# Two-layer graph kernel: ACT copies Wh from two PSUM banks, s is spread by TensorE, the masks of the first row group come ahead of the next products

## Chip, core and metric

One core of a Trainium2 chip runs the whole kernel in one launch. The metric is device time in microseconds; the median of three runs is compared.

## The reference

x is 8192x128, adj is 8192x8192 int32 of zeros and ones. Cut to what matters:

```python
Wh = x @ W;  s = Wh @ a1;  t = Wh @ a2            # layer 0: graph attention
e = s[:, None] + t[None, :]
e = where(e > 0, e, 0.2 * e);  e = where(adj > 0, e, -9e15)
x = layernorm(x + elu(softmax(e, axis=1) @ Wh))
x1 = adj @ x / adj.sum(axis=1)                    # layer 1: mean over neighbours
out = layernorm(x + concat([x1, x], 1) @ weight + bias)
```

## The kernel before

The 8192 rows are worked in 32 groups of 256 rows; two groups share one row block of 512 rows. The 8192 columns are 64 tiles of 128; 16 tiles are a chunk (four chunks to a group), 8 tiles are a half, and a half is one buffer of masks. The exponential of the leaky sum splits into a product of a row factor and a column factor, one pair for a positive sum and one for a negative sum, so that a group is two masked matmul sums: mask bits times `factors`, where `factors` holds per tile the column factor times Wh, as a float16 high part and a float16 rest.

**Start.** `turn_x(k)` on TensorE transposes four tiles of x, ACT copies them out of PSUM (`copy_turned`, L407), `make_wh(k)` (L563) multiplies by W and by the two vectors, so that Wh, s and t of four tiles land in two PSUM banks, two tiles in each. VectorE empties the banks (`copy_wh(k)`, L773: one copy of Wh and one of s and t per bank) and reduces the largest |Wh| (`largest_wh`, L784). There are sixteen such steps. Then TensorE transposes s and t (L601), ACT copies them, SyncE stores them to DRAM and reads s back, spread over the 128 partitions, for groups 0 and 1 (`load_s`, L238). VectorE and GpSimd find the maxima that scale the factors.

**Adjacency.** GpSimd's queue loads one chunk of 512 rows by 2048 columns per transfer (`load_adj`, L352); a buffer comes free when TensorE has packed it. `pack_bits(c)` (L583) packs 16 tiles into 16-bit words by 64 small matmuls, and ACT copies the words out (`copy_words`).

**Group 0.** It makes the factors as it goes. Per chunk VectorE makes two products (`make_product`, L828: column factor times Wh, one for each sign), ACT rounds each to float16 (L474, the high part), VectorE subtracts for the rest (`low_of`, L917) and makes the masks (`masks`, L880: four `unpack` instructions, two `negative`, two `positive`, from ACT's `scores`). VectorE's order by chunk is: rests of this chunk, products of the next chunk, masks of this chunk (L1039 to L1045). ACT's order by chunk is: two high parts, words, 16 scores (L471 to L484). `scores` is one instruction per tile of 128 columns. TensorE packs chunk c+1 and then multiplies the two halves of chunk c (`multiply`, L607), 32 matmuls each.

**Later groups.** TensorE multiplies from masks that VectorE and ACT make ahead. A group's first matmul waits until VectorE has scaled the sums of the group before out of PSUM (`add_negative`, L926, which comes with the masks of the second chunk). VectorE also joins the tiles of the next row block (`join`, L854), so that fewer matmuls pack them.

**Between the layers.** Every engine reads the flag `wide_flag` into a register (`is_wide`, L229) and jumps over a body that these inputs don't need; TensorE does so at L657, between the last group and the first block of layer 1. Layer 1 multiplies the whole adjacency from `words` once more.

Of the kernel before, what the change touches and what calls it, by code (L numbers as in the profile page):

```python
# [32 lines left out]
P = 128  # L33
BITS = 16
WPT = P // BITS
TPG = 2
# [22 lines left out]
def adj_resnorm_kernel(nc, x, adj, w0, a0, w1, b1, consts, out):  # L59
# [21 lines left out]
    with ctx:  # L81
# [73 lines left out]
        acc = [ctx.enter_context(nc.psum_tensor(f"acc{k}", [P, 512], F32)) for k in range(2 * TPG)]  # L155
# [7 lines left out]
        s_row_in = [sem("s_row_in0"), sem("s_row_in1")]  # L163
        rows_in, rows1_in = sem("rows_in"), [sem("rows1_in0"), sem("rows1_in1")]
# [67 lines left out]

        block = ctx.enter_context(nc.Block())
# [3 lines left out]
        def _(sp):  # L237
# [23 lines left out]
            load_s(0, 0)  # L261
            load_s(1, 1)
# [138 lines left out]
        def _(act):  # L401
# [19 lines left out]
            copy_turned(0)  # L421
            for k in range(1, NX):
                copy_turned(k)
            act.wait_ge(s_turned, 1)
# [6 lines left out]
            act.wait_ge(t_big_ok, 1)  # L431

            def scores(g, slot, h, first=False):

                if not (first and h < MASK_SLOTS):
                    act.wait_ge(mask_used, 8 * g + h + 1)
                    act.sem_inc(slot_free, 1)
# [16 lines left out]
            def group(g, slot, loads, next_words, before_last=None, second=False):  # L454

                act.wait_ge(s_row_in[slot], 16 * loads)
                for h in range(8):
                    scores(g, slot, h)
                    if second and h == UPG + 1:
                        act.wait_ge(wh_saved, 1)  # L460
                        act.wait_ge(e_low_ok, UPG)
                        act.wait_ge(f_low_ok, UPG)
# [8 lines left out]
            for c in range(UPG):  # L471
                for k in range(2):
                    act.wait_ge(product_ok, 2 * c + k + 1)
                    act.activation(factors[:, k, c * UNIT:(c + 1) * UNIT, 0:F], product[:, (2 * c + k) % 3, :, :],  # L474
                                   ACT.Copy)\
                        .then_inc(high_ok, 1)
                if c == 0:
                    act.wait_ge(s_row_in[0], 16)
                if c == 0:
                    copy_words(0, 0)  # L480
                for h in (2 * c, 2 * c + 1):
                    scores(0, 0, h, True)
                if c < UPG - 1:
                    copy_words(0, c + 1)  # L484
                if c == 0:
                    act.wait_ge(uy_ok, 2)
                    act.activation(u_col, uy_col, ACT.Exp).then_inc(exp_cols_ok, 1)
                    act.activation(v_col, vy_col, ACT.Exp).then_inc(exp_cols_ok, 1)
            group(1, 1, 1, {3: (1, 0)}, second=True)
            group(2, 0, 2, {0: (1, 1), 1: (1, 2), 3: (1, 3)}, before_last=True)  # L490
            group(3, 1, 2, {0: (2, 0), 1: (2, 1), 3: (2, 2)})
            with act.Fori(2, NR - 1) as n:
                group(PAIR * n, 0, n + 1, {1: (n, 3), 3: (n + 1, 0)})
                group(PAIR * n + 1, 1, n + 1, {1: (n + 1, 1), 3: (n + 1, 2)})
            group(NG - 2, 0, NR, {1: (NR - 1, 3)})
            group(NG - 1, 1, NR, {})
# [44 lines left out]
        def _(pe):  # L541
# [21 lines left out]
            def make_wh(k):  # L563

                pe.wait_ge(x_t_ok, k + 1)
                if k >= 2:
                    pe.wait_ge(wh_ok, k - 1)
                for j in range(XB):
                    o = (j % 2) * (F + 2)
                    m = pe.matmul(acc[2 * (k % 2) + j // 2][:, o:o + F + 2], x_t[:, k % 2, j * P:(j + 1) * P], wq,  # L570
# [12 lines left out]
            def pack_bits(c):  # L583

                pe.wait_ge(adj_in[c], 16)
                if c >= 2:
# [20 lines left out]
            def multiply(g, h, factors_in=False, first=False, pack_chunk=None):  # L607
# [3 lines left out]
                for a in range(2 * TPG):  # L611
                    b, neg = a // 2, a % 2
                    if factors_in and a < 2:
                        pe.wait_ge((e_low_ok, f_low_ok)[neg], h // 2 + 1)
# [25 lines left out]

            pe.wait_ge(den_hi_ok, 4)
            pe.wait_ge(edge_col_ok, 1)
            for c in range(UPG):
                if c < UPG - 1:
                    pack_bits(c + 1)
                for h in (2 * c, 2 * c + 1):
                    multiply(0, h, h % 2 == 0, True)
# [9 lines left out]
            with pe.If(is_wide(pe) > 0):  # L657
# [98 lines left out]
        def _(dve):  # L756
# [16 lines left out]
            def copy_wh(k):  # L773

                dve.wait_ge(wh_made, k + 1)
                j0 = XB * k
                for half in range(2):
                    bank = acc[2 * (k % 2) + half][:, 0:2 * (F + 2)].rearrange("p (j f) -> p j f", j=2)
                    dve.tensor_copy(wh[:, j0 + 2 * half:j0 + 2 * half + 2, :], bank[:, :, 0:F])  # L779
                    d = dve.tensor_copy(cols[:, 0:2, j0 + 2 * half:j0 + 2 * half + 2],  # L780
                                        bank[:, :, F:F + 2].rearrange("p j k -> p k j"))
                d.then_inc(wh_ok, 1)

            def largest_wh(k):  # L784

                dve.wait_ge(wh_ok, k + 1)
                dve.tensor_reduce(wh_top[:, k:k + 1], wh[:, XB * k:XB * (k + 1), :], AX.XY,  # L787
                                  ALU.max, apply_absolute_value=True).then_inc(top_ok, 1)

            for k in range(NX):  # L790
                copy_wh(k)
                if k < NX - 1:
                    largest_wh(k)
# [3 lines left out]
            largest_wh(NX - 1)  # L797
            dve.wait_ge(low_ok, 1)
# [439 lines left out]
```

## Time and profile before

| what | value |
|---|---|
| median of the runs | 1503.33 us (1502.51 to 1504.44) |
| profiled execution | 1502.18 us |
| its span, first to last instruction | 1500.5 us |
| TensorE busy | 1451.8 us |
| VectorE busy | 1006.9 us |
| ACT busy | 928.0 us |
| granted TensorE clock, mean | 0.985 |
| first matmul of group 1 | 102.76 us after the span's start |
| last matmul of layer 0, first of layer 1 | ends at 1006.69 us, starts at 1010.78 us |

All times of the rows are counted from the first instruction. A busy share of an engine is an average over the start, the groups and layer 1, which have different limits. Instructions of one engine overlap a little: 47 ACT instructions of 0.495 us each take 18.85 us, 0.40 us apart, so sums below go by the distance from start to start. Ends of matmuls are modelled.

### The profile page before, as it was taken

The page shows a single profiled execution, that of the slowest core. Times are in us where ns is not written, and L with a number is a line of the kernel's source. Part 1 is how long each engine was busy: PE and PEld are TensorE (multiplying, and loading weights), DVE is VectorE, ACT ScalarE, POOL GpSimd, SP SyncE. Part 2 cuts the span into 40 slices and gives each one's busy share as a digit, 9 for nine tenths or more (in the row PEclk, how much of TensorE's full clock was granted, in tenths as well). Part 3 has the DMA queues.
Part 4 walks back from the last instruction along what each step waited for, and adds up shares of the span by engine and source line. Part 5 has one row for each costly group of instructions (what it writes and reads, how often), then busy time and mean ns, then how long its engine had stood idle before and what let it go on. Part 6 is the DMA issues. An engine that isn't in the chain of part 4 may idle for free.

```text
span 1500.5 us, 33763 instructions
## 1 busy us (share of the span) xinstructions
PE 1451.8 (97%) x11974; PEld 1095.7 (73%) x11974; DVE 1006.9 (67%) x2878; ACT 928.0 (62%) x2272; POOL 118.3 (8%) x199
## 2 busy tenths in 40 slices
PE   7489999999999999999999999989999999999997
PEld 6378888888888888888888888874454545454543
DVE  7887888788888878888887888772433343334332
ACT  3799999999999999999999999940000000000000
POOL 1001100010010001001000100000000000000000
PEclk9699999999999999999999999999999999999999
DMA  9977998678778868886887782041000000000000
GB/s 170 113 75 81 119 108 96 84 87 96 93 79 96 93 85 88 95 93 80 95 95 84 87 96 37 19 114 48 21 15 21 14 21 14 21 14 21 14 14 14
DMA packets 99470, 101.68 MB, mean 68 GB/s; under 512 B 4448, under 2 KB 66656, under 8 KB 99424
## 3 DMA queue, kind: packets, MB, share of 16 engines
q0 software_dynamic: 33792, 67.11, 45.0%
q1 hardware_dynamic: 65632, 33.97, 8.7%
q8 instruction: 28, 0.46, 0.1%
q14 instruction: 18, 0.15, 0.0%
HBM read 289.74 MB, written 12.65 MB: 202 GB/s over the span
## 4 chain that ended last, share of the span: by engine, by line
PE 93%; DVE 2%; ACT 2%; DMA 1%; issue 1%; POOL 0%; SPq 0%; DVEq 0%; POOLq 0%; ACTq 0%
PE acc L622 60%; PE pack_ps L696 30%; ACT level_ring L439 1%; PE pack_ps L581 1%; PE turn_ps L718 1%; PE acc L731 1%; DVE words L779 1%; DVE wh_top L787 1%; DMA s_and_t<-words 1%; DMA s_row<-s_and_t 0%; PE turn_ps L707 0%; ACT factors L474 0%; DMA factors<-in_x 0%; PE acc L570 0%; DVE words L836 0%
## 5 line engine op out<-in xcount | busy, mean ns | idle before, releaser
L439 ACT ACTIVATE level_ring<-s_row,cols 128x256 fp8e4<-128x256 f32 x2048 | 829.5, 495 | 0.0
L622 PE MATMUL acc<-factors,edge_ring 128*128 128x259 f16 x4096 | 548.2, 274 | 20.5 <-DVE edge_ring L914 18.4
L622 PE MATMUL acc<-factors,level_ring 128*128 128x259 f16 x4096 | 547.8, 274 | 0.0
L696 PE MATMUL pack_ps<-adj_space,factors 128*128 128x512 fp8e4 x2048 | 452.4, 380 | 4.1 <-issue 4.1
L622 PEld LDWEIGHTS acc<-factors,edge_ring 128*128 128x128 fp8e4 x4096 | 365.7, 98 | 70.0 <-issue 21.2
L622 PEld LDWEIGHTS acc<-factors,level_ring 128*128 128x128 fp8e4 x4096 | 366.3, 98 | 48.6
L696 PEld LDWEIGHTS pack_ps<-adj_space,factors 128*128 128x128 f16 x2048 | 201.0, 98 | 237.1 <-issue 7.6
L907 DVE TENSOR_TENSOR level_ring<-level_ring,edge_ring 128x1024 uint16<-128x1024 uint16 x256 | 171.5, 690 | 110.0 <-ACT level_ring L439 99.7
L1073 DVE TENSOR_SCALAR adj_space<-words 128x512 uint16 (+1 forms) x448 | 96.4, 291 | 152.0 <-PE pack_ps L696 151.9
L581 PE MATMUL pack_ps<-pack_w,adj_space 128*128 128x32 bf16 x960 | 170.7, 178 | 0.0
L914 DVE TENSOR_TENSOR edge_ring<-edge_ring,level_ring 128x1024 uint16<-128x1024 uint16 x256 | 166.7, 684 | 0.0
L521 ACT ACTIVATE level_ring<-turn_ps 128x512 f32<-128x512 f32 x16 | 9.6, 598 | 229.6 <-PE turn_ps L707 229.6
L529 ACT ACTIVATE level_ring<-pack_ps 128x256 f32<-128x256 f32 x32 | 10.5, 381 | 226.8 <-PE pack_ps L696 226.8
L849 DVE TENSOR_SCALAR edge_ring<-words 128x512 uint16 (+1 forms) x448 | 106.6, 299 | 8.9 <-issue 6.4
L375 POOL TENSOR_SCALAR one<-mv 128x2 f32<-128x2 f32 x64 | 18.8, 294 | 1079.4 <-DVE mv L1010 1079.4
L581 PEld LDWEIGHTS pack_ps<-pack_w,adj_space 128*128 128x128 fp8e4 x960 | 91.6, 95 | 14.1
L1102 DVE SCALAR_TENSOR_TENSOR level_ring<-acc,cols,level_ring 128x128 f32<-128x128 f32 x64 | 19.5, 346 | 92.7 <-PE acc L731 92.6
L858 DVE SCALAR_TENSOR_TENSOR adj_space<-adj_space 128x1024 int32<-128x1024 int32 x60 | 73.2, 1220 | 0.0
L357 POOL DMA_DIRECT2D adj_space<-in_adj x64 | 51.4, 805 | 272.5 <-PE pack_ps L581 197.5
L418 ACT ACTIVATE words<-pack_ps 128x512 f32 (+1 forms) x64 | 38.2, 596 | 47.9 <-PE pack_ps L581 39.9
L377 POOL TENSOR_TENSOR one<-one 128x2 f32<-128x2 f32 x64 | 48.0, 749 | 9.5
L1015 DVE TENSOR_SCALAR level_ring<-level_ring,mv,one 128x128 f32<-128x128 f32 x64 | 19.3, 344 | 41.5 <-POOL one L377 41.5
(97 smaller groups left out, 651.4 us busy)
## 6 DMA issues: line engine op xcount, KB each, us to landing
adj_space<-in_adj POOLq DMA_DIRECT2D x64, 1024.0 KB, 14.4
factors<-in_x SPq DMA_DIRECT2D x8, 512.0 KB, 7.2
s_row<-s_and_t SPq DMA_DIRECT2D x32, 128.0 KB, 3.1
rows_x<-in_x SPq DMA_DIRECT2D x32, 128.0 KB, 2.1
x_rows<-rows_y SPq DMA_DIRECT2D x32, 128.0 KB, 9.8
x_parts<-parts SPq DMA_DIRECT2D x32, 128.0 KB, 4.4
factors<-x_parts SPq DMA_DIRECT2D x8, 512.0 KB, 4.5
level_ring<-x_rows SPq DMA_DIRECT2D x16, 256.0 KB, 2.8
```

The source lines that it names most:

```text
L357: pool.dma_start(adj_ring[:, c, :, :], adj_tiles[n, :, :, c * COLS:(c + 1) * COLS]).then_inc(adj_in[c], 16)
L377: pool.tensor_tensor(rstd, var_eps, minus_half, ALU.pow).then_inc(rstd_sem, TPG)
L418: act.activation(row_words[:, n, c * WPU:(c + 1) * WPU], pack_ps[c % 2][:, 0:WPU], ACT.Copy)\
L439: a = act.activation(level_bytes[:, h % MASK_SLOTS, j, :], s_row[:, slot, :], ACT.Relu, bias=t_big[:, h * HALF + j:h * HALF + j + 1], scal ...
L581: return pe.matmul(pack_ps[c % 2][:, j * WPR:(j + 1) * WPR], nibbles, pack_w[:, 0, :], start=True, stop=True)
L622: m = pe.matmul(acc[a][:, 0:WIDE_ROW], mask, factors[:, neg, jj, 0:WIDE_ROW], start=(jj == 0), stop=(jj == NJ - 1))
L696: m = pe.matmul(pack_ps[slot][:, :], factors[:, 0, jj, part * F:(part + 1) * F], ring_1_bytes[:, c, j, :], start=(jj == 0 and part == 0), ...
L849: d = dve.tensor_scalar(to, src, 6 - k, EDGES, ALU.logical_shift_left, ALU.bitwise_and)
L858: dve.scalar_tensor_tensor(out=pair[:, 0], in0=pair[:, 1], scalar=1, in1=pair[:, 0], op0=ALU.logical_shift_left, op1=ALU.bitwise_or).then_ ...
L907: dve.tensor_tensor(level, level, edge_ring[:, c % EDGE_SLOTS, k * HALF:(k + 1) * HALF, :], ALU.bitwise_and).then_inc(neg_ready, 1)
L914: dve.tensor_tensor(edges, edges, level_ring[:, (2 * c + k) % MASK_SLOTS, :, :], ALU.bitwise_xor)\
L1073: d = dve.tensor_scalar(to, src, 6 - k, EDGES, ALU.logical_shift_left, ALU.bitwise_and)
```

## The change

Wh leaves PSUM by one ACT instruction per step, over both banks; VectorE keeps one copy, of s and t. s of the first two groups is spread over the partitions by four matmuls and an ACT copy, and the two loads from DRAM go. ACT makes scores of group 0 from the start on, between its other work. VectorE's order by chunk of group 0 is rests, masks, next products. The last chunk's rests are made by halves of 8 tiles, each half followed by its masks. TensorE packs chunks 1 and 2 before the first multiplication, and reads the flag there.

```diff
 # ACT
+            def copy_wh(k):
+                act.wait_ge(wh_ok, k + 1)
+                act.activation(wh[:, XB * k:XB * (k + 1), :].rearrange("p (h j) f -> p h j f", h=2),
+                               wh_banks(k)[:, :, :, 0:F], ACT.Copy).then_inc(wh_copied, 1)
+            for k in range(NX):
                 copy_turned(k)
+                if k == 4:
+                    act.wait_ge(s_spread, 1)
+                    act.activation(s_row[:, :, :].rearrange("p k r -> p (k r)"), pack_ps[1][:, :], ACT.Copy)\
+                        .then_inc(s_row_ok, 1)
+                if k:
+                    copy_wh(k - 1)
+            copy_wh(NX - 1)
+            act.wait_ge(s_row_ok, 1)
+            first_scores(0, 4)
...
+            first_scores(4, 10)
...
+            copy_words(0, 0)
+            high_of(0)
+            high_of(1)
+            copy_words(0, 1)
+            first_scores(10, 30)
+            act.wait_ge(uy_ok, 2)
...
+            copy_words(0, 2)
+            high_of(2)
+            high_of(3)
+            first_scores(30, 50)
+            copy_words(0, 3)
+            high_of(4)
+            high_of(5)
+            first_scores(50, 64)
+            scores(1, 1, 0)
+            high_of(6)
+            high_of(7)
+            group(1, 1, 0, {3: (1, 0)}, second=True)
 # TensorE
                 if k >= 2:
-                    pe.wait_ge(wh_ok, k - 1)
+                    pe.wait_ge(wh_copied, k - 1)
...
+            def spread_s():
+                pe.wait_ge(wh_ok, 1)
+                for j in range(2 * TPG):
+                    m = pe.matmul(pack_ps[1][:, j * P:(j + 1) * P], s_col[:, j:j + 1].to_broadcast([P, P]), ident,
+                                  start=True, stop=True)
+                m.then_inc(s_spread, 1)
...
                 make_wh(k)
+                if k == 2:
+                    spread_s()
...
+            pe.wait_ge(wh_copied, NX)
+            pack_bits(1)
+            wide = is_wide(pe)
+            pack_bits(2)
             pe.wait_ge(den_hi_ok, 4)
             for c in range(UPG):
-                if c < UPG - 1:
-                    pack_bits(c + 1)
+                if c == 1:
+                    pack_bits(3)
...
-            with pe.If(is_wide(pe) > 0):
+            with pe.If(wide > 0):
 # VectorE
+            def copy_s_t(k):
                 dve.wait_ge(wh_made, k + 1)
+                dve.tensor_copy(cols[:, 0:2, XB * k:XB * (k + 1)].rearrange("p k (h j) -> p h j k", h=2),
+                                wh_banks(k)[:, :, :, F:F + 2]).then_inc(wh_ok, 1)
             for k in range(NX):
-                copy_wh(k)
-                if k < NX - 1:
-                    largest_wh(k)
+                copy_s_t(k)
+                if k:
+                    largest_wh(k - 1)
+                if k % XB == XB - 1 and k < NX - 1:
+                    scaled_t(k // XB)
...
+            def last_masks_of_first():
...
+                for k in range(2):
+                    low_half(2 * UPG - 2, k, e_low_ok)
+                    if k == 0:
+                        unpack(0, 0, UPG - 1, edge_ring, UPG - 1).then_inc(unpacked, 1)
+                    low_half(2 * UPG - 1, k, f_low_ok)
+                    negative(0, UPG - 1, k)
+                    positive(0, UPG - 1, k)
...
-            for c in range(UPG):
+            for c in range(UPG - 1):
                 low_of(2 * c, e_low_ok)
                 low_of(2 * c + 1, f_low_ok)
-                if c < UPG - 1:
-                    make_product(2 * c + 2)
-                    make_product(2 * c + 3)
                 masks(0, 0, c)
+                make_product(2 * c + 2)
+                make_product(2 * c + 3)
+            last_masks_of_first()
 # SyncE
-            load_s(0, 0)
-            load_s(1, 1)
```

`first_scores(a, b)` is the score instruction of tiles a to b-1 of group 0, and `high_of(n)` the rounding of product n. `wh_banks(k)` is the pair of banks of step k. `scaled_t(c)` scales t for 16 tiles; before, one instruction (L802) scaled all 64 at the end.

## Rows read from the trace of the kernel before

**Rows 1.** The page, part 1: engines' busy time, share of the span, instructions.

```profile
PE 1451.8 (97%) x11974; PEld 1095.7 (73%) x11974; DVE 1006.9 (67%) x2878; ACT 928.0 (62%) x2272; POOL 118.3 (8%) x199
```

**Rows 2.** TensorE's waits, 0 to 110 us: total, times, longest.

```profile
PE acc L622 <- DVE edge_ring L914: 18.4, 4, 12.9
```

**Rows 3.** TensorE's waits, 110 to 1500 us.

```profile
PE pack_ps L696 <- issue: 4.1, 1, 4.1
```

**Rows 4.** VectorE's waits, 38.5 to 102.7 us.

```profile
DVE level_ring L907 <- ACT level_ring L439: 6.6, 4, 2.5
DVE factors L922 <- ACT factors L474: 0.6, 1, 0.6
```

**Rows 5.** ACT's waits, 35 to 104 us.

```profile
ACT words L418 <- DMA s_row<-s_and_t: 6.1, 1, 6.1
```

**Rows 6.** Windows of VectorE: length, busy (instructions), clock, DMA share, GB/s.

```profile
10.00:35.30 25.30, 23.29 (x79) 1.00 1.10 162
35.30:38.58 3.28, 3.01 (x19) 0.65 1.07 107
38.58:102.61 64.03, 56.39 (x70) 0.78 1.02 108
```

**Rows 7.** Timeline of TensorE in the Wh steps: start, length, instruction.

```profile
13.33 1.06 PE L570 MATMUL acc<-words 128*128 128x130 f32 x8
...
14.66 1.06 PE L570 MATMUL acc<-words 128*128 128x130 f32 x8
```

**Rows 8.** Timeline of ACT in the Wh steps.

```profile
13.53 0.60 ACT L412 ACTIVATE words<-turn_ps 128x512 f32<-128x512 f32 x1 [0.98 <-PE turn_ps L560]
```

**Rows 9.** VectorE's lines, 10 to 35.3 us: busy, mean ns, idle before.

```profile
L779 DVE COPY words<-acc 128x256 f32<-128x256 f32 x32 | 13.1, 416 | 7.4 <-PE acc L570 7.4
L787 DVE TENSOR_REDUCE wh_top<-words 128x1 f32<-128x512 f32 x15 | 10.3, 686 | 0.5
L780 DVE COPY cols<-acc 128x4 f32<-128x4 f32 x32 | 4.9, 153 | 0.0
```

**Rows 10.** Timeline of group 0, all engines.

```profile
60.66 4.50 DVE L922 TENSOR_TENSOR factors<-words,factors 128x2048 f16<-128x2048 f32 x2 [0.61 <-ACT factors L474]
...
65.07 4.49 DVE L836 TENSOR_TENSOR words<-words,cols 128x2048 f32<-128x2048 f32 x2
...
69.47 0.90 DVE L849 TENSOR_SCALAR edge_ring<-words 128x512 uint16<-128x512 uint16 x4
...
70.91 3.70 ACT L474 ACTIVATE factors<-words 128x2048 f16<-128x2048 f32 x2
...
72.84 4.50 DVE L922 TENSOR_TENSOR factors<-words,factors 128x2048 f16<-128x2048 f32 x2
...
74.51 6.49 ACT L439 ACTIVATE level_ring<-s_row,cols 128x256 fp8e4<-128x256 f32 x16
...
84.63 1.89 PE L622 MATMUL acc<-factors,edge_ring 128*128 128x259 f16 x8 [3.34 <-DVE edge_ring L914]
...
102.13 0.48 DVE L936 TENSOR_SCALAR part_sums<-acc,cols 128x258 f32<-128x258 f32 x1
...
102.76 1.05 PE L622 MATMUL acc<-factors,edge_ring 128*128 128x259 f16 x8 [2.06 <-DVE part_sums L936]
```

**Rows 11.** Timeline between the layers.

```profile
1010.78 9.59 PE L696 MATMUL pack_ps<-adj_space,factors 128*128 128x512 fp8e4 x32 [4.09 <-issue]
...
1015.98 0.55 DVE L1185 RECIPROCAL cols<-cols 128x64 f32<-128x64 f32 x1 [1.17 <-issue]
```

**Rows 12.** Windows of all engines after the jump.

```profile
1010.70:1015.80 5.10, 5.02 (x12) 1.81 (x13) 2.19 (x8) 0.42 (x1) 0.92 (x2) 0.50 0.12 33
```

**Rows 13.** DMA queues, 1008.0 to 1008.2 us: packets, MB, share.

```profile
q8 instruction: 1, 0.02, 36.9%
```

**Rows 14.** GpSimd's timeline at the first adjacency loads.

```profile
16.22 3.17 POOL L357 DMA_DIRECT2D adj_space<-in_adj  x4 [15.25 <-DMA factors<-in_x]
```

**Rows 15.** Adj_space, 0 to 140 us: its transfers.

```profile
DMA to landing us min/median/max: 13.4/22.3/42.7
```

More of the change, by code:

```diff
@@ L152, in adj_resnorm_kernel @@
                          for k in (1, 2))
-        acc = [ctx.enter_context(nc.psum_tensor(f"acc{k}", [P, 512], F32)) for k in range(2 * TPG)]
+        acc_banks = ctx.enter_context(nc.psum_tensor("acc", [P, 2 * TPG, 512], F32))
+        acc = [acc_banks[:, k, :] for k in range(2 * TPG)]
         pack_ps = [ctx.enter_context(nc.psum_tensor(f"pack_ps{k}", [P, 512], F32)) for k in range(2)]
@@ L430, in _, with scores @@
             act.activation(f_col, t_col, ACT.Exp, bias=neg_ft, scale=ALPHA).then_inc(exp_cols_ok, 1)
[L431 to L437, printed above, removed]
+            first_scores(4, 10)
+            def scores(g, slot, h):
+                act.wait_ge(mask_used, 8 * g + h + 1)
+                act.sem_inc(slot_free, 1)
                 for j in range(HALF):
@@ L454, in group @@
             def group(g, slot, loads, next_words, before_last=None, second=False):
-                act.wait_ge(s_row_in[slot], 16 * loads)
+                if not second:
+                    act.wait_ge(s_row_in[slot], 16 * loads)
                 for h in range(8):
-                    scores(g, slot, h)
+                    if h or not second:
+                        scores(g, slot, h)
                     if second and h == UPG + 1:
                         act.wait_ge(wh_saved, 1)
-                        act.wait_ge(e_low_ok, UPG)
-                        act.wait_ge(f_low_ok, UPG)
+                        act.wait_ge(e_low_ok, UPG + 1)
+                        act.wait_ge(f_low_ok, UPG + 1)
                     if h == UPG and not second:
@@ L468, in group @@
                         exponential(g - 1)
-            for c in range(UPG):
[L472 to L482, printed above, removed]
-                if c < UPG - 1:
[L484 to L488, printed above, removed]
@@ L489, in _, with high_of @@
-            group(1, 1, 1, {3: (1, 0)}, second=True)
-            group(2, 0, 2, {0: (1, 1), 1: (1, 2), 3: (1, 3)}, before_last=True)
-            group(3, 1, 2, {0: (2, 0), 1: (2, 1), 3: (2, 2)})
+            def high_of(n):
+                act.wait_ge(product_ok, n + 1)
+                act.activation(factors[:, n % 2, (n // 2) * UNIT:(n // 2 + 1) * UNIT, 0:F], product[:, n % 3, :, :],
+                               ACT.Copy).then_inc(high_ok, 1)
+            copy_words(0, 0)
+            high_of(0)
@@ L492, in _ @@
+            scores(1, 1, 0)
+            high_of(6)
+            high_of(7)
+            group(1, 1, 0, {3: (1, 0)}, second=True)
+            group(2, 0, 1, {0: (1, 1), 1: (1, 2), 3: (1, 3)}, before_last=True)
+            group(3, 1, 1, {0: (2, 0), 1: (2, 1), 3: (2, 2)})
             with act.Fori(2, NR - 1) as n:
[L493 to L495 removed]
@@ L496, in _ @@
-            group(NG - 1, 1, NR, {})
+                group(PAIR * n, 0, n, {1: (n, 3), 3: (n + 1, 0)})
+                group(PAIR * n + 1, 1, n, {1: (n + 1, 1), 3: (n + 1, 2)})
+            group(NG - 2, 0, NR - 1, {1: (NR - 1, 3)})
+            group(NG - 1, 1, NR - 1, {})
             high_parts(NG - 2)
@@ L924, in low_of, with low_half @@
                     .then_inc(done, 1)
+            def low_half(n, k, done):
+                c, part = n // 2, n % 2
+                js = slice(c * UNIT + k * HALF, c * UNIT + (k + 1) * HALF)
+                dve.wait_ge(high_ok, n + 1)
+                dve.tensor_tensor(factors[:, part, js, FD:FD + F], product[:, n % 3, k * HALF:(k + 1) * HALF, :],
+                                  factors[:, part, js, 0:F], ALU.subtract).then_inc(done, 1)
             def add_negative(g, first=False):
```

46 lines of the change are left out of this document (28 added, 18 removed).

## The prediction

> **What bounds the kernel now.** The page's busy times come first: TensorE works 1451.8 us of the span of 1500.5 [rows 1], so a change counts only where TensorE stands still, or where something else comes before its work. Its waits by stretch say where that is. Before 110 us it waits 18.4 us for VectorE's masks of group 0 [rows 2]. After 110 us it has one long stop, 4.1 us at the change from layer 0 to layer 1 [rows 3]. So the groups from 1 on are one unbroken chain of TensorE: what starts group 1 earlier ends the kernel earlier by as much, if nothing new stops TensorE on the way.
>
> Group 1's first matmul starts at 102.76 us, released by VectorE's scaling of the first sums at 102.13 [rows 10]. In the start it is thus VectorE that is late. Its waits and windows tell how its time goes: from the first product at 38.58 to the scaled sums at 102.61 it is busy 56.39 us of 64.03 [rows 6], and waits 6.6 us for ACT's scores and 0.6 us for ACT's high parts [rows 4]; the remaining 0.4 us are small hand-overs. ACT in its turn stood 6.1 us for the s rows from DRAM [rows 5]. Before 38.58 VectorE is busy 23.29 of 25.30 us in the Wh steps [rows 6], so it bounds these too.
>
> **Wh steps.** Sixteen steps keep VectorE 23.29 us, 1.46 each. Where it did not yet hold TensorE back, a step took 1.33 us (13.33 to 14.66 [rows 7]). The change takes two Wh copies of 0.416 us and one small copy of 0.153 out of VectorE's step [rows 9]; 0.153 + 0.686 = 0.84 us are left, below 1.33. ACT gets a second instruction of 128x512 a step. No row has one over two banks: from below it is the 0.60 us that the same number of values takes from one bank [rows 8], from above 1.20, as two instructions. I take 0.60, the nearest row in shape. Two of 0.60 are 1.20 us a step, and consecutive ACT instructions overlap, which covers the short accumulator read that follows each transposed copy; so TensorE paces. At 1.20 it would be ACT, with 1.80 a step. A step's results are now handed on twice, from VectorE to ACT and on, but to a matmul two steps later, 2.66 us, in which 0.15 + 0.60 of copies, 0.60 of the next transposed copy and 1.06 of matmuls fit closely (2.41).
>
> `spread_s` adds four float32 matmuls of nearly the size of those in a step, 1.06 us as a row, 1.0 taken. The ACT copy of s adds 0.60 once, in the slack. From step 2 at 13.33, step 15 starts at 13.33 + 13 x 1.33 + 1.0 = 31.6, ends at 32.7, and s and t are out at 32.9; before, 35.3. VectorE then has one `largest_wh` (0.69) left that it used to have done, and afterwards the same small instructions, 3.28 us [rows 6]: the first product starts at 32.9 + 0.69 + 3.28 = 36.9 instead of 38.58. **Gain 1.7 us.** At the old pace of 1.46 it is nothing; with 1.80 a step it is 13 x 0.47 = 6.1 less, a loss of 4.4. Those are the ends.
>
> **Group 0 on VectorE.** Its instructions stay: eight products and eight rests (4.41 us a pair, from 60.66 to 65.07 and on to 69.47), five mask sets of 3.37 (69.47 to 72.84) [rows 10], one join, one scaling. Splitting the last two rests adds two instructions; half of a rest plus a little more makes 0.15 us in all. The order changes what it waits for. The 0.6 us for high parts and the 6.6 us for scores go, if ACT keeps ahead: the s rows are in SBUF from step 4, ten scores are made before the first high part, thirty by the time of the second chunk, all 64 and the first eight of group 1 before the last two high parts.
>
> Whether ACT keeps ahead is the close point. A score takes 6.49 / 16 = 0.40 us, a pair of high parts 3.7 [rows 10]. Between the end of one chunk's products and the end of the next chunk's first product VectorE needs 4.41 + 3.37 + 2.2 = 10.0 us. In that time ACT has a high part (1.9), 20 scores (8.0) and a copy of words (0.60, taken from the equal size in rows 8), 10.5 us. So it is late by 0.5, of which 0.3 are covered, because the rest waits for the high part only after one more product (2.2 against 1.9). In the last chunk 22 scores make 8.8 and the total 10.7 without the words: late by 0.7, uncovered 0.5. I add 0.9 us for chunks 2 and 3 together. Lower end 0, upper end 3 (19 changes of work on ACT at 0.15 each, should none overlap).
>
> From first product to scaled sums: 64.03 - 7.2 + 0.15 + 0.9 = 57.9 us, so 36.9 + 57.9 = 94.8 instead of 102.61. **Gain 7.8 us with the Wh steps.**
>
> **TensorE and the transfers in group 0.** TensorE must not become last. It packs chunk 2 before its first multiplication, and so waits for that transfer. The four first transfers are issued from 16.22 within 3.17 us [rows 14]; the first lands 13.4 us later, near 29.6, the last 42.7 us after an issue near 18.6, at 61.3 [rows 15]. Evenly spaced, the third lands near 50.7. The engines' share of over 1 in these windows [rows 6] leaves no room for earlier ones, though the two s loads are gone. Packing takes about 2 us, so TensorE starts near 52.7; the first mask is there at 36.9 + 4.4 + 1.4 (small columns) + 4.4 + 3 = 50.1. That costs nothing: a chunk is 64 matmuls, 8.4 us by rows of eight at 1.05 without their overlap [rows 10], some 11 where the clock is low, against VectorE's 12.2. The two last halves end near 92, 2.7 us ahead of 94.8; that is the price at which the cover ends. Behind this wait stand only masks that TensorE takes in order. On GpSimd's queue the next transfers are issued when a buffer is packed, and are served in turn, so nothing asked for in group 1 comes later than before.
>
> SyncE loses two loads; its store of s stays and nobody waits for it now in the start. The flag is read where TensorE waits for the transfer: free.
>
> **Between the layers.** Of the 4.09 us [rows 11] the wait and read of the flag go, the jump stays. VectorE passes its own read and jump with an idle 1.17 us [rows 11], which bounds a read by the nearest row from above; the ends for TensorE are 0 and 4.09. I take 1.0. Then 3.1 us of standing remain. After a stop of 3.34 us eight matmuls took 1.89 us, after one of 2.06 us 1.05 [rows 10]; after 4.09 us the granted clock was 0.50 for 5.1 us [rows 12], the lower of the two levels, and half of that, 2.55 us, is what it cost. 3.1 is nearer to 3.34, so I leave this cost in.
>
> In the gap, 1.3 us after the last matmul's modelled end, an instruction queue moved 0.02 MB [rows 13]; whose, the row doesn't say. The Trainium skill (Runtime: NRT & Kernel Launch, "Instruction fetch mechanics") has it that a taken branch to code outside the fetched window must first bring that code by DMA. By that rule the jump is the gap, the gain here is 0 and the time 1.0 us longer; by VectorE's row it is 1.0.
>
> **Sum.** 7.8 + 1.0 = 8.8 us from the profiled execution's 1502.18 (1.7 of it outside the span): 1493.4. The median of the runs was 1.15 above that execution, so 1494.5 is what I predict for the median.
>
> **Rivals.** (1) *ACT bounds group 0.* From 33.5 to near 81.5 its list is 72 scores (28.8), eight high parts (14.8), four copies of words (2.4) and the small exponentials, about 47 of 48 us. Against it: these are full durations that overlap. Price up to 3 us: 1497.5. (2) *The gap between the layers stays*, since it is the jump: 1495.5. (3) *The gap falls to about 2 us* and the clock holds: 1.0 us less of standing than forecast and 2.55 less at the low clock, 1491.0. For it: a stop of 2.06 us didn't lower it; against it: the read would have to be 2 us, above VectorE's 1.17. (4) *The change doesn't speed up the Wh steps*: the two-bank copy costs 1.20, or the hand-overs stretch the step; 1496.2 at the old pace, 1500.6 at 1.80 a step. (5) *Slower:* TensorE's code is longer at the start, and its loops' bodies come to lie elsewhere. If a turn of a loop then had to wait for code as the jump does, each of the 13 turns in layer 0 and 7 in layer 1 would cost 4.09 - 1.17 = 2.9 us: 58 us, 1552. It outweighs the gain from 0.44 us a turn. For it: the gap at the jump. Against it: no turn costs anything now [rows 3].
>
> **How the numbers follow.** Chances: forecast 0.45, rival 1 0.2, rival 2 0.15, rival 3 0.12, rival 4 0.05, rival 5 0.03. The range goes from 1490.5 (rival 3 with ACT never late) to 1498.5 (rival 1 with 1 us of the Wh steps lost); what it leaves out is rival 5, the bad half of 4 and the tails. 0.2%, 3 us, is about what a measurement here can tell from no change. All cases but rival 5 and the worst of 4 lie below 1500.3: faster 0.94, same 0.03, slower 0.03.
>
> **What would show it.** The first matmul of group 1 near 95 us; Wh steps 1.33 us apart; VectorE's waits for ACT in group 0 about 1 us in place of 7.2; ACT with no wait for a transfer; TensorE with no wait between 97 us and the end of layer 0; a gap near 3 us after it. Wrong is the prediction if VectorE waits for high parts at every chunk, if TensorE still has masks to wait through after VectorE's scaling, or if TensorE stops at loop turns.

## The result, and the profile after

The changed kernel took 1488.42 us (median of four runs, 1487.8 to 1490.44); the kernel before, run beside it, 1503.6 (1502.51 to 1504.44). The ratio is 0.9902, with a 95% interval of 0.989 to 0.9913. Forecast were 1494.5 us and a range of 1490.5 to 1498.5: the direction was right, and the gain about 6 us too small. The profiled execution of the changed kernel took 1488.95 us against 1502.18.

TensorE still fills the span (page, part 1; against [rows 1]):

```profile
span 1487.2 us, 33752 instructions
...
PE 1449.8 (97%) x11982; PEld 1095.5 (74%) x11982; DVE 995.0 (67%) x2835; ACT 936.7 (63%) x2289; POOL 118.2 (8%) x199
```

TensorE's waits from 0 to 110 us (total, times, longest; against [rows 2]) and VectorE's from 36 to 93.5 us (against [rows 4]):

```profile
PE pack_ps L627 <- DMA adj_space<-in_adj: 8.2, 2, 7.8
PE acc L668 <- DVE edge_ring L981: 5.6, 2, 5.1
...
PE acc L668 <- DVE part_sums L1011: 2.4, 1, 2.4
```

```profile
DVE factors L998 <- ACT factors L502: 0.3, 1, 0.3
```

TensorE waits for masks 5.6 us instead of 18.4, and newly 8.2 us for adjacency transfers; VectorE, which waited 7.2 us for ACT, now waits 0.3. The windows of VectorE (length, busy, clock, DMA share, GB/s; against [rows 6]) cut the start at the end of the Wh steps, the first product and the scaled sums:

```profile
10.00:32.40 22.40, 11.71 (x34) 1.00 1.12 173
32.40:36.05 3.65, 3.01 (x21) 0.88 1.06 107
36.05:93.33 57.28, 56.37 (x72) 0.80 1.06 111
```

In the Wh steps VectorE is now half idle; from the first product on its busy time is the old one (56.37 against 56.39) in 57.28 us instead of 64.03. ACT's copy of Wh over two banks takes 0.60 us (against [rows 8], one bank):

```profile
18.65 0.60 ACT L427 ACTIVATE words<-acc 128x512 f32<-128x512 f32 x1 [0.16 <-DVE cols L826]
```

TensorE's timeline (start, length, instruction, idle before; against [rows 7] and [rows 10]) shows both ends of the start, and the passage to layer 1 (against [rows 11]):

```profile
17.35 1.06 PE L604 MATMUL acc<-words 128*128 128x130 f32 x8
...
18.68 1.06 PE L604 MATMUL acc<-words 128*128 128x130 f32 x8
...
49.39 1.89 PE L627 MATMUL pack_ps<-pack_w,adj_space 128*128 128x32 bf16 x64 [7.77 <-DMA adj_space<-in_adj]
51.12 1.57 PE L668 MATMUL acc<-factors,edge_ring 128*128 128x259 f16 x8
...
90.02 1.05 PE L668 MATMUL acc<-factors,level_ring 128*128 128x259 f16 x8
93.47 1.89 PE L668 MATMUL acc<-factors,edge_ring 128*128 128x259 f16 x8 [2.40 <-DVE part_sums L1011]
95.16 1.76 PE L668 MATMUL acc<-factors,level_ring 128*128 128x259 f16 x8
96.76 1.05 PE L668 MATMUL acc<-factors,edge_ring 128*128 128x259 f16 x8
...
997.87 1.05 PE L668 MATMUL acc<-factors,level_ring 128*128 128x259 f16 x8
999.73 5.55 PE L746 MATMUL pack_ps<-adj_space,factors 128*128 128x512 fp8e4 x25 [0.81 <-issue]
```

The window of all engines behind that passage (against [rows 12], granted clock 0.50) has the clock at full:

```profile
999.70:1004.00 4.30, 4.27 (x20) 1.98 (x21) 3.47 (x13) 0.42 (x1) 0.00 (x0) 1.00 0.36 106
```

Four differences of these timelines make up the 13.3 us by which the span is shorter:

- Group 1 starts at 93.47 instead of 102.76: 9.29 us.
- Its first 16 matmuls run at the low clock after a stop of 2.40 us. They are 1.69 and 1.60 us apart by eights, where 0.885 is usual. From there to the layer's last matmul it takes 905.45 us instead of 903.93: 1.52 lost.
- The stop between the layers is 0.81 instead of 4.09: 3.28.
- No low clock follows it. From layer 1's first matmul to the end of the span it takes 487.47 instead of 489.72: 2.25.

The last two come to 5.5 us, 3.28 and 2.25. The forecast had 1.0 for them.

### The profile page after: what moved, and what is told of

It reads as the page before. It is cut to its first block, busy times and chain, and to the rows that moved or that the text cites. A ratio compares the mean times of both kernels' runs of the same rounds, so it can differ in the third digit from the quotient of the medians.

```text
span 1487.2 us, 33752 instructions
## 1 busy us (share of the span) xinstructions
PE 1449.8 (97%) x11982; PEld 1095.5 (74%) x11982; DVE 995.0 (67%) x2835; ACT 936.7 (63%) x2289; POOL 118.2 (8%) x199
## 4 chain that ended last, share of the span: by engine, by line
PE 92%; DVE 1%; DMA 0%; issue 0%; POOL 0%; ACT 0%; SPq 0%; DVEq 0%; POOLq 0%; ACTq 0%
PE acc L668 60%; PE pack_ps L746 29%; PE pack_ps L615 1%; PE turn_ps L768 1%; PE acc L781 1%; PE turn_ps L757 0%; DMA level_ring<-x_rows 0%; POOL one L380 0%; DMA x_parts<-parts 0%; DVE stats L1078 0%; DVE edge_ring L981 0%; DVE level_ring L1177 0%; DVE adj_space L913 0%; DVE mv L1085 0%; DVE level_ring L1090 0%
## 5 line engine op out<-in xcount | busy, mean ns | idle before, releaser
L465 ACT ACTIVATE level_ring<-s_row,cols 128x256 fp8e4<-128x256 f32 x1984 | 803.7, 495 | 0.0
```

## Experiments

Each edit is made in the changed kernel unless it says otherwise. Times are medians; "ratio" is to the kernel before, run beside it, with its 95% interval.

### The flag of the jump

**e1: TensorE's read of the flag back to its old place, right before the jump.**

```diff
-            wide = is_wide(pe)
             pack_bits(2)
 ...
-            with pe.If(wide > 0):
+            with pe.If(is_wide(pe) > 0):
```

> The changed kernel with TensorE's read of the flag put back between the layers, nothing else. Theory A (the read itself stops TensorE for most of the 4.09 us, and the stop lowers the clock): the gap is again near 4.1 us, the clock is 0.50 for some 5 us after it, and the kernel takes 3.3 + 2.3 = 5.6 us more, 1494.0, ratio to before 0.9938. Theory B (the jump is the gap; it got shorter because other code lies there): the gap stays near 0.8 us, time 1488.4, ratio 0.990. Theory C (the read costs as much as on VectorE, 1.0 to 1.2 us, the rest is something else): gap near 2.0 us, clock kept, 1489.5.

1494.73 us (1492.73 to 1495.44), ratio 0.9943 (0.9929 to 0.9957): 6.3 us above the changed kernel; in the profiled executions 0.6 of that is a later start of group 1 (94.09 us).

**e2: the kernel before, with nothing changed but that read**, put behind the first packing.

```diff
             pack_bits(0)
+            wide = is_wide(pe)
 ...
-            with pe.If(is_wide(pe) > 0):
+            with pe.If(wide > 0):
```

> The kernel before with only TensorE's read of the flag moved into the start, behind the packing of chunk 0. Theory A: the gap between the layers falls from 4.09 to near 0.8 us, the clock stays up, 5.6 us less, 1498.0, ratio 0.9963; group 1 still starts near 102.8 us. Theories B and C: at most 1.2 us less, 1502.4, ratio 0.9992.

1498.09 us, ratio 0.997 (0.9959 to 0.9981), 5.2 us below before. TensorE's timelines at the first matmul of layer 1, e1 and then e2:

```profile
998.64 1.05 PE L668 MATMUL acc<-factors,level_ring 128*128 128x259 f16 x8
1004.03 8.27 PE L745 MATMUL pack_ps<-adj_space,factors 128*128 128x512 fp8e4 x26 [4.34 <-issue]
```

```profile
1005.55 1.05 PE L623 MATMUL acc<-factors,level_ring 128*128 128x259 f16 x8
1008.48 6.85 PE L697 MATMUL pack_ps<-adj_space,factors 128*128 128x512 fp8e4 x31 [1.88 <-issue]
```

With the late read the stop is 4.34 us, and 26 matmuls take 8.27: the low clock. With the early one it is 1.88, and 31 take 6.85: the full clock. Taken out alone (e1) or put in alone (e2), the read's early place is worth about 5 to 6 us, and the same two terms carry it in the traces: 3.5 us of the stop and 2.2 of the clock in e1, 2.2 and 2.5 in e2. That is shown. What a read costs is not yet.

**e10 and e12: reads added among the groups**, e10 with one and two, e12 with four and eight in the same places. The diff is e10's.

```diff
             group(1, {1: (1, 0), 2: (1, 1), 3: (1, 2)})
+            is_wide(pe)
             group(2, {1: (1, 3), 2: (2, 0), 3: (2, 1)})
+            is_wide(pe)
+            is_wide(pe)
```

> The changed kernel with TensorE reading the flag again where no jump follows: once between groups 1 and 2, twice in a row between groups 2 and 3. Theory A (the read itself stops TensorE, wherever it stands): a stop of 2.4 to 3.5 us before group 2, and near 5 to 7 us before group 3, if the two follow one another, each with the lower clock behind it; 10 to 14 us more, 1500. Theory K (TensorE's sequencer reads ahead while matmuls run, and the stop between the layers came from read and jump together): stops under 1 us, 1489.5.

> The changed kernel with four reads of the flag on TensorE in a row before group 2 and eight before group 3. Theory M (TensorE's sequencer is some time ahead of the matmuls, a read takes part of that lead, and only what exceeds the lead is a stop): with a read of r us and a lead of R us the stops are 4r - R and 8r - R; from the runs so far 2r is below R and r plus the jump's code above it, so at r = 1.2 and R = 3.5 stops of 1.3 and 6.1 us. Theory N (a read never stops TensorE, only a jump that hangs on a fresh read does): no stop at either place.

e10: 1488.53 us (ratio 0.9908, 0.9892 to 0.9925), and TensorE stops at neither place. A read by itself is therefore not what costs 4 us, as I had taken it. e12, one run of 1495.59 (before: 1502.73), has stops at both:

```profile
124.39 1.05 PE L668 MATMUL acc<-factors,edge_ring 128*128 128x259 f16 x8 [1.34 <-issue]
...
158.08 1.89 PE L668 MATMUL acc<-factors,edge_ring 128*128 128x259 f16 x8 [3.96 <-DVE edge_ring L985]
```

The profile puts the second down to a mask, but VectorE had made the masks of group 3's first chunk by 150.4 us, and in e13 TensorE starts that group 3.9 us before the same mask is made; so the reads are left. Four more of them add 2.62 us, 0.66 each; four stop TensorE for 1.34, so the sequencer was some 1.3 us ahead of the matmuls, which two reads just use up, as in e10. These are estimates from two stops.

**e11: TensorE's part for wide inputs left out, and with it the jump. e13: a short jump on a fresh read before group 2, one on the early read before group 3.**

```diff
-            with pe.If(wide > 0):
-                pe.sem_inc(w_sum, 2)
 ...
```

```diff
             group(1, {1: (1, 0), 2: (1, 1), 3: (1, 2)})
+            with pe.If(is_wide(pe) > 0):
+                pe.sem_inc(sums_read, 1)
             group(2, {1: (1, 3), 2: (2, 0), 3: (2, 1)})
+            with pe.If(wide > 0):
+                pe.sem_inc(sums_read, 1)
```

> The changed kernel without TensorE's body for wide inputs and the jump over it (left out: what TensorE does when the flag is set). Theory A: the gap between the layers, 0.8 us, is the jump; it falls to 0.1 to 0.2 us, 0.7 us less, 1487.7. Theory L (the gap is the change from one kind of matmul to the other and the waits before it): the gap stays at 0.6 to 1.0 us.

> The changed kernel with two short jumps on TensorE among the groups, each over a single semaphore instruction that isn't executed: before group 2 with a fresh read of the flag, before group 3 with the flag read at the start. Theory M: neither stops TensorE by more than 0.3 us, since a short jump needs no code from elsewhere and the lead covers one read. Theory N: a stop of 2.4 to 3.5 us before group 2, none before group 3.

e11: 1489.88 us (ratio 0.9916, 0.99 to 0.9933), no idle time at all between the layers. But e10 and e12 keep the jump and have none there either, and c1, the changed kernel once more, has 0.51 us instead of 0.81, so e11 doesn't show that the 0.81 us are the jump. The time did not fall. In e11 TensorE waits further on instead, for a transfer that layer 1's first transposes need:

```profile
1014.13 0.66 PE L729 MATMUL turn_ps<-consts_sb,level_ring 128*128 128x128 f32 x4 [1.14 <-DMA level_ring<-x_rows]
```

In every kernel of these runs whose stop between the layers is at most 1.3 us, these transposes start 14.9 to 15.2 us after layer 0's last matmul. So the last 1 us or so of the stop is free: without it TensorE waits for the transfer.

e13: one run, 1487.53 (before: 1502.73), no stop at either place. So neither the read nor a jump on a fresh read cost anything there, where the jump is short.

**e14: the read one group ahead of the jump, some 28 us. e15: two reads right before it.**

```diff
             group(NG - 2, {})
+            wide = is_wide(pe)
             group(NG - 1, {})
```

```diff
+            is_wide(pe)
+            with pe.If(is_wide(pe) > 0):
```

> The changed kernel with TensorE's read one group ahead of the long jump, before the last group, some 28 us early. Theory P (the long jump's code can be fetched ahead only when the flag is known in time; a read right before it puts read and fetch behind the last matmuls): the gap between the layers is 0 to 1.9 us, as with the read at the start, and the clock stays up; 1488. Theory Q (the gap belongs to this place in the code, whatever is read where): 4 us or more, 1494.

> Like e1 (read right before the long jump), with one more read in front of it. From e12 a read is 0.66 us of the sequencer's time, so the gap of e1, 4.34 us, becomes 5.0 if read and code fetch follow one another and nothing is hidden any more (theory P); 4.3, if the second read is covered by the lead.

One run each, beside 1501.49 before: 1487.36 and 1495.53. The timelines of e14 and e15:

```profile
997.79 5.56 PE L746 MATMUL pack_ps<-adj_space,factors 128*128 128x512 fp8e4 x25 [0.56 <-issue]
```

```profile
1004.09 6.16 PE L746 MATMUL pack_ps<-adj_space,factors 128*128 128x512 fp8e4 x16 [4.25 <-issue]
```

One group of lead is enough; how much less would do was not run. A second late read adds nothing to the stop (4.25 against e1's 4.34), where I had expected about 5: it is not the read's 0.66 us that makes the stop long.

What moves is a transfer of code. An instruction queue brings one piece of 0.02 MB shortly before layer 1 starts, as in [rows 13]; the queues of 997.0 to 997.2 us in the changed kernel, of 1001.2 to 1001.4 in e1, and of 997.1 to 997.3 in e11, which has no jump (queue, packets, MB, share):

```profile
q8 instruction: 1, 0.02, 33.0%
```

```profile
q8 instruction: 1, 0.02, 36.2%
```

```profile
q8 instruction: 1, 0.02, 48.0%
```

With the jump it comes at a nearly fixed distance ahead of the first matmul of layer 1, 2.4 to 2.8 us, in before (1008.1 to 1010.78), e1 (1001.3 to 1004.03), e2 (1006.0 to 1008.48), e14 (995.3 to 997.79), e15 (1001.4 to 1004.09) and the changed kernel (997.1 to 999.73). To TensorE's last matmul of layer 0 it stands differently. With the late read it comes 1.4 us behind that matmul's end in before (1006.69) and 1.6 in e1 (999.69). With the early one it comes 1.8 ahead in the changed kernel (998.92) and 0.6 ahead in e2 (1006.60).

The reading that fits: the first matmul behind the long jump waits for this piece, some 2.6 us from its start, with either read. If the flag is known, the sequencer gets to the jump while the last matmuls run, and most of the transfer lies beside them. That the read's place moves the stop is shown by e1, e2 and e14; that it does so through this transfer is argued from the distances. No row says whose code the piece is, and in e11 one comes at 997.2 us without any jump, 1.8 us ahead of layer 1's first matmul. Over the whole execution e11 brings 26 such pieces, the changed kernel 28.

This is the Trainium skill's rule (Runtime: NRT & Kernel Launch, "Instruction fetch mechanics") that a taken branch out of the fetched window waits for its code by DMA. The fixed distance agrees with it.

**Open:** why the late read moves the transfer by 3.4 us (1.8 ahead to 1.6 behind), when a read elsewhere costs an estimated 0.66 beyond its lead and a short jump on a fresh one cost nothing.

### The start

**e7: the s rows of the first two groups from DRAM again.**

```diff
             sp.wait_ge(s_out, 16)
+            load_s(0, 0)
+            load_s(1, 1)
 ...
-                if k == 2:
-                    spread_s()
 ...
-            first_scores(0, 4)
 ...
-            first_scores(4, 10)
 ...
-            first_scores(10, 30)
+            act.wait_ge(s_row_in[0], 16)
+            first_scores(0, 30)
```

> The changed kernel with the s rows of the first two groups read back from DRAM as before; no spreading by TensorE, all 64 scores of group 0 behind the words of chunk 1 and the transfer. Theory I (the s rows were what group 0 waited for): the rows come near 48, VectorE's first masks 6.5 us later, chunk 1 some 2 us more by ACT's list, group 1 starts near 102.4; 9 us more than the changed kernel, 1497.4, ratio 0.996. Theory J (ACT has slack enough to make the scores up before the last chunk): 4 us more at most, 1492.4.

1499.12 us (1498.05 to 1500.19), ratio 0.9969 (0.9957 to 0.9981): 10.7 us worse than the changed kernel. VectorE's waits from 36 to 103 us and TensorE's first matmuls of group 1:

```profile
DVE level_ring L967 <- ACT level_ring L437: 7.1, 2, 4.6
DVE factors L982 <- ACT factors L497: 1.8, 1, 1.8
```

```profile
102.84 1.05 PE L661 MATMUL acc<-factors,edge_ring 128*128 128x259 f16 x8 [2.41 <-DVE part_sums L1004]
```

VectorE's wait for scores is back, and group 1 starts where it did before the change. Without the early s rows the rest of the change gains nothing in the start. The experiment also moves ACT's first 30 scores behind the words of chunk 1, as it must, so it prices the rows and the early scores together. In the traces group 1's start costs 9.4 us, of which 1.5 come back because the clock stays up there; another 2.5 are lost between the layers, in a stop of 1.95 us and at the low clock behind it.

**e4: the Wh copies on VectorE again, one copy for s and t kept.**

```diff
-                if k:
-                    copy_wh(k - 1)
-            copy_wh(NX - 1)
 ...
+                for half in range(2):
+                    d = dve.tensor_copy(wh[:, XB * k + 2 * half:XB * k + 2 * half + 2, :], wh_banks(k)[:, half, :, 0:F])
+                d.then_inc(wh_copied, 1)
```

> The changed kernel with the Wh copies back on VectorE (two of 128x256 a step, behind its copy of s and t); ACT copies no Wh. Theory D (VectorE's chain decides group 1's start): a Wh step takes 1.5 us again instead of 1.33, the first product comes 2 to 2.6 us later, group 1 starts near 95.8, 2.3 us more than the changed kernel, 1490.7, ratio 0.9917. Theory G (the start of group 0 is set by ACT's list or by the adjacency transfers, so the Wh steps don't count): group 1 starts as in the changed kernel within 0.5 us, 1488.4, ratio 0.990.

1488.31 us (1487.62 to 1488.46), ratio 0.9896 (0.9881 to 0.9911): no loss in the median. VectorE's timeline in a Wh step:

```profile
21.27 0.17 DVE L823 COPY cols<-acc 128x8 f32<-128x8 f32 x1
21.34 0.75 DVE L826 COPY words<-acc 128x256 f32<-128x256 f32 x2
22.00 0.68 DVE L832 TENSOR_REDUCE wh_top<-words 128x1 f32<-128x512 f32 x1
22.60 0.17 DVE L839 TENSOR_SCALAR cols<-cols 128x16 f32<-128x16 f32 x1
```

The two large copies and the small one take 0.73 us, from 21.27 to 22.00, and the reduction 0.60 more until the next small instruction at 22.60: 1.33, and TensorE's rows of eight in that stretch stand 1.33 apart as well (21.44 and 22.77). So one small copy less takes VectorE's step from 1.46 to TensorE's pace. That ACT's copy is worth nothing is not shown by this. In e4's trace the first product comes at 36.80 us and group 1 at 94.23, 0.76 later than in the changed kernel, but the clock stays up there, which gives back 1.5. Other kernels with the changed start begin group 1 between 93.31 (e14) and 94.23 (e15), so 0.76 can't be told from the spread either.

**e5: products ahead of the masks again in the first three chunks. e6: the last chunk whole** (with the counts that wait for its rests).

```diff
-                masks(0, 0, c)
                 make_product(2 * c + 2)
                 make_product(2 * c + 3)
+                masks(0, 0, c)
```

```diff
-            for c in range(UPG - 1):
+            for c in range(UPG):
 ...
-            last_masks_of_first()
```

> The changed kernel with VectorE's old order in chunks 0 to 2: next products ahead of this chunk's masks; ACT's order stays. Theory D (VectorE does the same work without waits in either order, and its scaling decides): each chunk's masks come 4.4 us later, TensorE is behind until the last chunk and ends group 0 near 94 without a stop before group 1; time within 1 us of the changed kernel, 1488, ratio 0.990. Theory H (the order itself brings part of the gain): 3 to 4.4 us more, 1492, ratio 0.9925.

> The changed kernel with the last chunk of group 0 made whole (rests of 16 tiles, then both masks), as the other chunks. Theory D (VectorE's scaling decides group 1's start, not TensorE's end of group 0): VectorE's scaled sums come at the same time within 0.3 us, 93.2; TensorE ends group 0 near 93.5 instead of 91.1, with no stop of 2.4 us and no lower clock in group 1; 1.0 to 1.5 us less, 1487.2. Theory F (the halves are worth the time by which TensorE ends group 0 earlier, as the change intends): 2.4 us more, 1490.8.

e5: 1490.38 us (1489.67 to 1490.96), ratio 0.9912 (0.9897 to 0.9927). The time is 2 us up. VectorE waits for ACT 1.5 us instead of 0.3, but it isn't last: TensorE waits 6.3 us for the masks of chunk 2 (counted from 0), until 80.05, and from there works without a stop into group 1, which starts at 95.91 instead of 93.47. The clock that stays up there gives back 1.5. e6: 1489.61 (1488.68 to 1490.3), ratio 0.9911 (0.9896 to 0.9927), between what the two theories gave. In e6 TensorE is last, as its timeline shows:

```profile
87.45 1.35 PE L668 MATMUL acc<-factors,edge_ring 128*128 128x259 f16 x8 [3.85 <-DVE edge_ring L981]
88.60 1.94 PE L668 MATMUL acc<-factors,level_ring 128*128 128x259 f16 x8
...
96.21 1.05 PE L668 MATMUL acc<-factors,edge_ring 128*128 128x259 f16 x8
```

It begins the last chunk only at 87.45, at the low clock at first, and VectorE's scaling waits for it a little. Group 1 follows at 96.21, 2.7 us later than in the changed kernel, but without the stop of 2.40 us and its low clock. So 1.5 of the 2.7 us that the halves gain are lost again at the low clock: the medians differ by 1.2 us, within the two ranges.

### The stop before group 1

**e3 and e9: VectorE's join behind the masks of a group's second chunk**, in e3 for group 1, in e9 for groups 1 to 3. Before, it stood ahead of the scaling, which releases the next group. The diff is e9's.

```diff
-                if 0 in joins:
+                late = isinstance(n, int) and n < 2
+                if 0 in joins and not late:
                     join(*joins[0])
                 masks(n, q, 1, "sums", second)
+                if 0 in joins and late:
+                    join(*joins[0])
```

> The changed kernel with VectorE's first join (1.91 us) moved behind the masks of group 1's second chunk, so that the scaling of group 0's sums comes before it. Theory D (VectorE's order decides group 1's start, and the stop of 2.40 us there costs another 1.5 us by the lower clock): TensorE ends group 0 at 91.1, the scaled sums come at 91.5, group 1 starts near 91.6 instead of 93.47, its first 32 matmuls take 0.11 us each; 1.9 + 1.5 = 3.4 us less, 1485.0, ratio 0.9877. Theory E (the time is only shifted: group 1's later masks or its packing come late instead): the same as the changed kernel, within 1 us, with new waits of TensorE after 95 us.

> The changed kernel with the joins that precede the scaling put behind the masks of the second chunk in groups 1, 2 and 3 (in e3 only in group 1, where TensorE then waited 1.1 us at the start of group 3, because VectorE stood before the scaling for an adjacency transfer). Theory D with that cause: group 1 starts near 91.6 to 92.4 with no lower clock, and the wait of 1.1 us at group 3 is gone; 3 us less than the changed kernel, 1485.4, ratio 0.988. Theory E (the transfers of the second row block give the time back wherever the join stands): a wait of 1 us or more of TensorE for the packing between 130 and 190 us, and the time of e3, ratio 0.9896.

e3: 1486.97 us (1486.8 to 1487.96), ratio 0.9896 (0.988 to 0.9911). TensorE's start of group 1, and VectorE's timeline at group 3:

```profile
92.45 1.05 PE L668 MATMUL acc<-factors,edge_ring 128*128 128x259 f16 x8 [0.54 <-DVE part_sums L1011]
```

```profile
150.31 1.23 DVE L913 SCALAR_TENSOR_TENSOR adj_space<-adj_space 128x1024 int32<-128x1024 int32 x1 [1.12 <-DMA adj_space<-in_adj]
```

The stop falls from 2.40 to 0.54 us and the clock stays up. But the next joins come earlier against their transfers: VectorE waits 1.12 us for one, with group 3's release behind it, and TensorE waits 1.1 us there. e9 moves those joins as well: **1485.78 us (1485.51 to 1486.16), ratio 0.9881 (0.9866 to 0.9897)**, the fastest version, 2.6 us below the changed kernel. Its stop at group 1:

```profile
91.47 1.05 PE L668 MATMUL acc<-factors,edge_ring 128*128 128x259 f16 x8 [0.55 <-DVE part_sums L1011]
```

No wait of TensorE is left from there to the passage between the layers. The runs of e9 lie below all those of the changed kernel (1487.8 to 1490.44) and of c1; e3's overlap with them.

**c1: the changed kernel once more**, to see if the low clock at group 1 comes back.

> The changed kernel itself, unaltered, in the same company as the two runs beside it. Ratio 0.990 within 0.0012. If the lower clock at group 1's start depends on how the stop of 2.4 us happens to lie, the first 16 matmuls of group 1 take 1.05 us by eight in this profile, and group 1 ends 1.5 us sooner after its start than in the first profile; if a stop of 2.4 us always lowers the clock, they take 1.89 and 1.76 again.

1488.53 us (1487.62 to 1489.68), ratio 0.9905 (0.9889 to 0.9922). It does here, but not in all kernels that stop as long (last section):

```profile
93.56 1.89 PE L668 MATMUL acc<-factors,edge_ring 128*128 128x259 f16 x8 [2.36 <-DVE part_sums L1011]
```

## Why the prediction failed

**The step that failed is "Between the layers".** It took 1.0 us for the flag, from VectorE's idle 1.17 us [rows 11], and left the low clock in. Measured are 3.28 us of the stop and 2.25 of the clock, 5.5 in all. Three things were wrong in it. VectorE's passage, though the nearest row, was no bound for TensorE's. The sum "read plus jump" was the wrong form: a read is 0.66 us by the estimate from e12 and stops nothing by itself (e10), and the jump on a flag read early leaves 0 to 1.95, while the two together stop TensorE for 4.1 to 4.3; what counts is whether the flag is read right before the jump (e1, e15) or at least a group ahead (e14). And the wait for code, by which I had put the gain at 0 in rival 2, need not be a stop: TensorE can work beside it, as the distances above suggest. Why the late read costs as much as it does stays open. Rival 3 came nearest: its mechanism, a shorter stop after which the clock holds, is what happened, with a stop of 0.81 where it had about 2.

With this term at 5.5 the sum is 7.8 + 5.5 = 13.3, the difference of the two spans. On the profiled executions the forecast was 1493.4 against 1488.95. The other 1.7 us of the 6.1 are the step to the medians: I had added 1.15, and the median after lay 0.5 below its execution.

**The start: 7.8 us net, as forecast, but by two errors that cancel.**

- *Wh steps.* They stand 1.33 us apart, as forecast, and ACT's copy over two banks takes 0.60, the lower end. That ACT takes the large copies from VectorE was not needed for this pace (e4). The first product came at 36.05 for 36.9. Other executions with this start have it at 35.4 to 36.8 us, all a little earlier than forecast.
- *Group 0.* From first product to scaled sums 57.28 us for 57.9. ACT's lateness, taken at 0.9, was 0.3: rival 1 did not occur. e7 shows that without the early s rows and scores nothing of the gain is left. The working's own terms for ACT's lateness, 0.2 and 0.5, make 0.7 where it added 0.9.
- *TensorE and the transfers.* The third transfer let packing begin at 49.39 and multiplication at 51.12, for 52.7; group 0 ended at 91.07 for 92. That cost nothing, as said.
- *Group 1's start* was 93.47, for a little over 94.8. But with TensorE done at 91.07, it now stood 2.40 us for VectorE, and the clock fell: 1.52 us. The prediction named this margin ("2.7 us ahead of 94.8") as cover and never asked what a stop of that length does there, though it priced the clock at the jump.

**Rivals 2, 4 and 5** did not occur: the stop fell, the Wh steps sped up, and from 97 us to the end of layer 0 TensorE waits for nothing, and in layer 1 once, for 0.6 us, so no loop turn had to wait for code. The range's lower end does not come out of its parts: rival 3 with ACT never late is 1490.1, not 1490.5.

## What to carry to other kernels

Read what decides a far jump well ahead of it: here that is worth 5 to 6 us, the shorter stop and the clock that is kept together, and one group of lead is enough. Put what releases the next group ahead of work that nobody waits for yet (the joins, 2.6 us), and look at all groups where the order is moved, since the next wait sits behind the same work. A term is bounded by rows of the engine that it is about, and the clock is priced at every stop that a change makes, not at the longest one alone.

## What the runs showed of the hardware

A stop of the same length lowers TensorE's clock in some executions and not in others. At group 1's start, stops of 2.36 to 2.41 us lowered it to the lower of its two levels in five profiles (the changed kernel, c1, e1, e11, e15) and left it up in six (e4, e7, e10, e12, e13, e14), for example in e10:

```profile
93.53 1.05 PE L668 MATMUL acc<-factors,edge_ring 128*128 128x259 f16 x8 [2.40 <-DVE part_sums L1014]
```

Up to that place e10, e12 and e13 have the changed kernel's own code. In e4 even 3.41 us, ahead of chunk 2 of group 0, left the clock up for all 64 matmuls behind it:

```profile
74.69 1.05 PE L665 MATMUL acc<-factors,edge_ring 128*128 128x259 f16 x8 [3.41 <-DVE edge_ring L981]
```

Before the change 3.34 us had lowered it at once [rows 10]. In e7 it fell late: after 3.42 us the first eight matmuls ran at the full clock and the next at the low one:

```profile
83.12 1.05 PE L661 MATMUL acc<-factors,edge_ring 128*128 128x259 f16 x8 [3.42 <-DVE edge_ring L974]
84.00 1.69 PE L661 MATMUL acc<-factors,level_ring 128*128 128x259 f16 x8
```

So the length of the stop alone doesn't decide it; what else does, the runs do not settle. At group 1 the low clock costs about 1.5 us. The four runs of c1 lie at 1487.6, 1487.7, 1489.4 and 1489.7 us, a spread of that size within one kernel; the low clock is known only for the profiled one of 1489.36, so that it makes the spread is not shown.

The stop of the long jump with the flag known early is not fixed either: 0 in e10 and e12, 0.51 in c1, 0.81 in the changed kernel, 1.88 in e2, 1.95 in e7. In e7 the clock fell behind it (0.50 from 1010 to 1012 us), in e2 it did not. That is the spread to reckon with in a term of this kind.
